# Routing weights kept on chip, gathers paced, row transpositions in the rounded type, and a new order inside the softmax attentions

## The reference

```
x = LN(x + attention(x))          # 16 heads on 4 key heads, softmax            phase "gqa"
x = LN(x + latent_attention(x, ctx)); x = LN(x + ternary_ffn(x))                # "latent", "ternary"
x = LN(x + decayed_linear_attention(x))                                        # phase "decay"
x = LN(x + cross_attention(x, ctx))   # 16 heads, causal softmax                 phase "causal"
x = LN(x + shared_ffn(x) + sum over the 2 best of 8 experts of score[e] * expert_ffn[e](x))   # "shared", "expert"
```

## Time and profile before

| | |
|---|---|
| median of 3 runs | 2088.39 us |
| the profiled execution: its time, its span | 2087.5 us, 2085.7 us |
| mean granted clock of TensorE | 0.967 |
| busy: PE, PEld | 1887.3 us (90%), 1535.6 us (74%) |
| busy: DVE, ACT, POOL | 1041.1 us (50%), 713.2 us (34%), 385.6 us (18%) |
| phases, start of each (us): gqa, latent, causal, shared, expert | 0, 272, about 1298, 1533, 1772 |
| the last TensorE product ends | 2041.0 us |

### The profile page before, as it was taken

The page is one execution under the profiler, slowest core; times in us unless marked ns, Lnnn a source line. Parts: engine busy times, 40 slices in busy tenths (PEclk is TensorE's granted clock), DMA queues, the critical chain, the costliest instruction groups (busy, mean ns, idle before and its releaser), DMA issues. The chain is left out here.

```text
span 2085.7 us, 32789 instructions
## 1 busy us (share of the span) xinstructions
PE 1887.3 (90%) x12124; PEld 1535.6 (74%) x12124; DVE 1041.1 (50%) x1836; ACT 713.2 (34%) x2275; POOL 385.6 (18%) x339
## 2 busy tenths in 40 slices
PE   8899888999999989999899998899879995999991
PEld 6667566788888767777677776677658874899990
DVE  5666753455555446333364547677865332222224
ACT  3555624334444332111231102545632210233332
POOL 1111100000000038000021100001104322745335
PEclk9999999999999999999999999999999998999995
DMA  7110142000000022000093000000015100644257
GB/s 238 42 46 14 43 160 82 1 1 1 1 1 1 1 76 91 1 0 0 24 352 115 1 20 27 26 2 1 2 46 207 46 0 0 243 149 143 82 114 205
DMA packets 73375, 135.89 MB, mean 65 GB/s; under 512 B 13456, under 2 KB 31760, under 8 KB 71184
## 3 DMA queue, kind: packets, MB, share of 16 engines
q1 hardware_dynamic: 47376, 96.28, 13.3%
q0 software_dynamic: 7888, 27.94, 4.5%
q10 hardware_dynamic: 17968, 9.71, 1.8%
HBM read 90.62 MB, written 43.29 MB: 64 GB/s over the span
## 5 line engine op out<-in xcount | busy, mean ns | idle before, releaser
L1473 PE MATMUL banks<-ternary_xth,ternary_wq 128*128 (+1 forms) x352 | 140.6, 399 | 5.0 <-DVE ternary_wq L1404 3.6
L1473 PE MATMUL banks<-ternary_xtl,ternary_wq 128*128 (+1 forms) x352 | 139.4, 396 | 0.0
L97 PE MATMUL banks<-latent_vh,latent_cth 128*128 128x512 f32 x256 | 104.2, 407 | 3.5 <-DVE latent_ctl L1174 3.5
L97 PE MATMUL banks<-weights,expert_xgh 128*128 x312 | 104.7, 336 | 2.4 <-DVE expert_xgl L2086 2.4
L99 PE MATMUL banks<-weights,expert_xgl 128*128 x312 | 101.6, 326 | 0.0
L573 ACT ACTIVATE gqa_pr<-banks,gqa_nb 128x128 f32<-128x128 f32 x256 | 90.4, 390 | 32.6 <-DVE gqa_nb L715 32.6
L98 PE MATMUL banks<-weights,expert_xgh 128*128 x312 | 101.4, 325 | 0.0
L573 ACT ACTIVATE causal_pr<-banks,causal_nb 128x128 f32<-128x128 f32 x256 | 90.4, 395 | 31.1 <-DVE causal_nb L715 31.1
L99 PE MATMUL banks<-latent_vh,latent_ctl 128*128 128x512 f32 x256 | 100.1, 391 | 0.0
L98 PE MATMUL banks<-latent_vl,latent_cth 128*128 128x512 f32 x256 | 100.1, 391 | 0.0
L1433 DVE TENSOR_TENSOR ternary_hf<-ternary_sg,banks 128x512 f32<-128x512 f32 x44 | 30.2, 687 | 135.4 <-issue 79.5
(11 more groups left out here) (462 smaller groups left out, 5412.0 us busy)
## 6 DMA issues: line engine op xcount, KB each, us to landing
x_slots<-decay_zeros SPq DMA_DIRECT2D x39, 256.0 KB, 4.3
y_slots<-decay_zeros SPq DMA_DIRECT2D x39, 256.0 KB, 4.5
y_slots<-expert_ys SPq DMA_DIRECT2D x39, 256.0 KB
expert_xin<-x_slots SPq DMA_DIRECT2D x38, 256.0 KB, 2.9
weights_raw<-in_expert_experts SPq DMA_DIRECT2D x4, 2176.0 KB, 9.2
gqa_tw<-in_ternary_w ACTq DMA_DIRECT2D x4, 2112.0 KB
ternary_raw<-in_ternary_w SPq DMA_DIRECT2D x11, 768.0 KB, 4.1
expert_raw<-in_expert_experts POOLq DMA_DIRECT2D x3, 2176.0 KB, 9.7
```

The costliest lines, as they stand in the source:

```text
L97: pe.matmul(out, wh, xh, start=first, stop=False, **kw)
L1473: a = pe.matmul(dst[:, :], wq[:, j, m, c * P:(c + 1) * P], x[:, c, toks], start=c == 0 and n == 0, stop=c == C - 1 and n == 1)
```

## The change

Scores are no longer scattered: `s_slots`, its zeroing, its 32 scatters in the shared phase and the 39 loads of scores in the expert phase go. ScalarE's `store` copies without a scale, and VectorE multiplies by the score, which is still in SBUF, as it adds a gathered row. For that the lower slots are now gathered into buffers rather than added into `X` by the DMA, with at most two gathers in flight, and VectorE adds them; an upper gather goes into the same buffer and waits until the lower one has been added. The row transpositions of tiles 1 to 38 are done in `F32R`, through an identity that ScalarE rounds at the start of the phase. In the softmax attentions, `rec` and `lo` move ahead of `S`, and `T` (b-1, 1) moves behind `out` (b-2).

```diff
         for b in range(B + 2):
             for h in range(2):
+                if soft and h == 0 and 1 <= b <= B:
+                    plan.append(("rec", b - 1, 0))
+                if soft and h == 0 and b >= 2:
+                    plan.append(("lo", b - 2, 0))
                 if b < B and (h == 0 or not soft):
                     plan.append(("S", b, h))
-                if soft and h == 0 and b >= 2:
-                    plan.append(("lo", b - 2, 0))
...
                 if soft:
-                    if h == 0 and 1 <= b <= B:
-                        plan += [("T", b - 1, 1), ("rec", b - 1, 0)]
                     if h == 0 and b >= 2:
                         plan.append(("out", b - 2, 0))
                     if h == 0 and 1 <= b <= B:
-                        plan.append(("rt", b - 1, 0))
+                        plan += [("T", b - 1, 1), ("rt", b - 1, 0)]
...
-            for n in range(2 * B):
-                at = bass.IndirectOffsetOnAxis(ap=S.pos[:, n:n + 1], axis=0)
-                if n and n % 2 == 0:
-                    pool.wait_ge(scored, 16 * n)
-                pool.indirect_dma_start(S.s_slots, at, S.score[:, n:n + 1], None).then_inc(scored, 16)
-            pool.wait_ge(scored, 16 * 2 * B)
...
             for t in range(B):
-                pool.indirect_dma_start(S.X[:, t, :], None, S.y_slots, slots(t), compute_op=ALU.add).then_inc(low_added[t], 16)
+                if t >= 2:
+                    pool.wait_ge(low_in[t - 2], 16)
+                pool.indirect_dma_start(yg[t], None, S.y_slots, slots(t)).then_inc(low_in[t], 16)
             pool.wait_ge(y_out[(TILES - 1) % 2], 16 * ((TILES - 1) // 2 + 1))
             for t in range(B):
+                pool.wait_ge(low_added, t + 1)
                 pool.indirect_dma_start(yg[t], None, S.y_slots, slots(B + t)).then_inc(yg_in[t], 16)
...
-                act.wait_ge(s_in[i % NX], 16 * (i // NX + 1))
-                act.activation(ys[:, i % 2, :], yb[i % 2], ACT.Copy, scale=sc[:, i % NX:i % NX + 1]).then_inc(y_copied, 1)
+                act.activation(ys[:, i % 2, :], yb[i % 2], ACT.Copy).then_inc(y_copied, 1)
+            act.activation(identr[:, :], S.ident[:, :], ACT.Copy).then_inc(ident_rounded, 1)
...
+            def add_scored(n, k):
+                x = S.X[:, n, :]
+                return dve.scalar_tensor_tensor(out=x, in0=yg[n], scalar=S.score[:, k * B + n:k * B + n + 1], in1=x,
+                                                op0=ALU.mult, op1=ALU.add)
+            for n in range(B):
+                dve.wait_ge(low_in[n], 16)
+                add_scored(n, 0).then_inc(low_added, 1)
...
                     dve.wait_ge(yg_in[n], 16)
-                    dve.tensor_tensor(S.X[:, n, :], S.X[:, n, :], yg[n], ALU.add).then_inc(high_added, 1)
+                    add_scored(n, 1).then_inc(high_added, 1)
...
                 for c in range(C):
-                    m = pe.transpose(tr[:, c * P:(c + 1) * P], x[:, c * P:(c + 1) * P], S.ident[:, :])
+                    cols = slice(c * P, (c + 1) * P)
+                    if i:
+                        m = pe.transpose(tr[:, cols].bitcast(F32R), xin[:, i % NX, cols], identr[:, :])
+                    else:
+                        m = pe.transpose(tr[:, cols], S.first_x[:, cols], S.ident[:, :])
```

More of the change, by code:

```diff
@@ L443, in _ @@
                         sp.dma_start(rows, zeros[:, :]).then_inc(slots_zero, 16)
-                sp.dma_start(S.s_slots.rearrange("(p i) n -> p (i n)", p=P), zeros[:, 0:TILES]).then_inc(slots_zero, 16)
-                sp.wait_ge(slots_zero, 32 * (SLOTS // P) + 16)
+                sp.wait_ge(slots_zero, 32 * (SLOTS // P))
                 sp.dma_start(next_c, S.ctx_dram[:, 0:GT, :]).then_inc(next_c_in, 16)
@@ L1557, in shared_ffn_phase @@
         route_in, given_done, ranked = sem("route_in"), sem("given_done"), sem("ranked")
-        slots_done, rows_done, scattered, scored = sem("slots_done"), sem("rows_done"), sem("scattered"), sem("scored")
+        slots_done, rows_done, scattered = sem("slots_done"), sem("rows_done"), sem("scattered")
         gw_in, gw_zero, first_x_in = sem("gw_in"), sem("gw_zero"), sem("first_x_in")
@@ L1929, in expert_ffn_phase @@
         weh, wel = S.weh, S.wel
-        xin = sb("xin", [P, NX, DM])
+        xin, identr = sb("xin", [P, NX, DM], F32R), sb("identr", [P, P], F32R)
         yg = [raw[t // 8][:, (t % 8) * DM:(t % 8 + 1) * DM] for t in range(B)]
@@ L1935, in expert_ffn_phase @@
         ys = sb("ys", [P, 2, DM])
-        sc = sb("sc", [P, NX])
         six, mv = sb("six", [P, B, 6]), sb("mv", [P, B, 2])
@@ L1945, in expert_ffn_phase @@
         y_out = [sem(f"y_out{b}") for b in range(2)]
-        s_in = [sem(f"s_in{b}") for b in range(NX)]
-        low_added = [sem(f"low_added{b}") for b in range(B)]
+        low_in = [sem(f"low_in{b}") for b in range(B)]
         yg_in = [sem(f"yg_in{b}") for b in range(B)]
-        high_added = sem("high_added")
+        low_added, high_added = sem("low_added"), sem("high_added")
         w_hi, w_ready, tile_done, spare_set = sem("w_hi"), sem("w_ready"), sem("tile_done"), sem("spare_set")
+        ident_rounded = sem("ident_rounded")
         tr_full, tr_hi, tr_lo = sem("tr_full"), sem("tr_hi"), sem("tr_lo")
@@ L1966, in load @@
             def load(i):
-                sp.dma_start(xin[:, i % NX, :], rows(S.x_slots, i)).then_inc(x_in[i % NX], 16)
-            def load_score(i):
-                sp.dma_start(sc[:, i % NX:i % NX + 1], rows(S.s_slots, i)).then_inc(s_in[i % NX], 16)
+                sp.dma_start(f32(xin[:, i % NX, :]), rows(S.x_slots, i)).then_inc(x_in[i % NX], 16)
             for i in range(1, NX):
                 load(i)
-            for i in range(NX):
-                load_score(i)
             for e in (1, 2):
@@ L1983, in _ @@
                 sp.dma_start(rows(S.y_slots, i), ys[:, i % 2, :]).then_inc(y_out[i % 2], 16)
-                if i + NX < TILES:
-                    load_score(i + NX)
             for t in range(B):
@@ L2115, in _ @@
                 if n < B:
-                    dve.wait_ge(low_added[n], 16)
                     dve.wait_ge(yg_in[n], 16)
-                    dve.tensor_tensor(S.X[:, n, :], S.X[:, n, :], yg[n], ALU.add).then_inc(high_added, 1)
+                    add_scored(n, 1).then_inc(high_added, 1)
                 if 1 <= n <= B:
@@ L2141, in transposes @@
                 if i:
+                    pe.wait_ge(ident_rounded, 1)
                     pe.wait_ge(x_in[i % NX], 16 * (i // NX + (i % NX > 0)))
                     pe.wait_ge(tr_lo, i)
-                x = xin[:, i % NX, :] if i else S.first_x
                 for c in range(C):
-                    m = pe.transpose(tr[:, c * P:(c + 1) * P], x[:, c * P:(c + 1) * P], S.ident[:, :])
+                    cols = slice(c * P, (c + 1) * P)
[3 more added lines that the diff above has]
+                        m = pe.transpose(tr[:, cols], S.first_x[:, cols], S.ident[:, :])
                 m.then_inc(tr_full, 1)
@@ L2219, in build @@
         S.landed_at = sb("landed_at", [P, E], U32)
-        S.s_slots = nc.dram_tensor("s_slots", (SLOTS, 1), F32).ap()
         S.ring, S.owner1 = sb("ring", [P, TILES], U32), sb("owner1", [P, TILES], U32)
```

## The result

On one chip the changed kernel took 2092.19 us (median of 13, 2084.73 to 2096.08) and the kernel before 2085.87 (median of 13): ratio **1.0027**, 95% interval 1.0017 to 1.0037. So it is slower by 0.27%, inside the half per cent called "no change" above, but on the other side of zero from the -0.7 us of the sum. The profiled execution of the changed kernel took 2088.54 us with a span of 2086.7 (before: 2087.5 and 2085.7). It lies 3.7 us under its kernel's median and the one of before 1.6 us over its own, so the two traces differ by 1.0 us where the medians differ by 6.3.

What follows compares the result with a forecast made beforehand. TensorE, busy 90% of the span, was taken as the bound; boundary -18.0, its clock -1.0, transpositions -3.8, order +16.1 and its clock +6.0 gave -0.7 on 2087.5: 2086.8 us, forecast as 2087, range 2060 to 2102.

Steps and rivals of the forecast that it cites:

- the sum: All priced terms added, against the profiled 2087.5 us: -18.0 - 1.0 - 3.8 + 16.1 + 6.0 = -0.7 us.
- The boundary: Between shared and expert phase: without POOL's score scatters, TensorE's 20.9 us stall falls to about 3 us, -18.0 us.
- the transpositions: Expert phase: four row transpositions in the rounded type take 0.34 us for 0.44, over 38 tiles -3.8 us.
- what hides: Score loads, zeroing of `s_slots`, ScalarE's copy without a scale and its identity rounding: hidden beside other work, 0.
- the clock behind the boundary: Start of the expert phase: less half clock after the shorter stall, -1.0 us (between 0 and -2.7).
- the rule for weight loads: Expert transpositions: loading 128 columns takes 107 ns, so no saving and 3.8 us longer; as a rival 0.14, 2090.6 us.
- The mechanism of the order: Softmax phases: 22.5 us of waits for the spread go; TensorE waits for `rts` and the probabilities' copy instead.
- the first path: Softmax steps: late `T` delays the second-half exponentials that overwrite what it reads, and `rts` with them, by 1.8 us.
- the size of the order in the attentions: Both softmax phases: +16.1 us of waits (ends -22.5 and +24) and +6.0 us of clock (0 to +12).
- the seven that the sum had priced: Softmax k and v steps and gqa's 11: new stalls of about 3 us, priced within the +6.0 us of clock.
- 10.6: Steps 12 to 15 of both softmax phases, without projections to cover the copy: 10.6 us for 10.0, +4.8 us.
- POOL's new waits are met early: At the end, POOL's waits before the upper gathers are met 1 to 6 us early, costing 0.

Runs made afterwards that it cites:

- e8: The changed kernel with the expert phase's row transpositions back in plain float32: 2093.55 us, ratio 1.0055 to the kernel before.
- e1: The changed kernel with the old order of the softmax phases, all else as changed: 2064.41 us, ratio 0.9881 to the kernel before.
- e5: The changed kernel with a third buffer in the causal phase, so second-half exponentials don't wait for `T`: 2075.81 us, ratio 0.9953 to the kernel before.
- e3: The changed kernel with `T` (b-1, 1) back ahead of `out`, `rec` and `lo` still ahead of `S`: 2048.19 us, ratio 0.9791 to the kernel before.
- e14: The changed kernel with `T` (b-1, 1) behind `out` only from step 12 on: 2070.55 us, ratio 0.9945 to the kernel before.
- e13: The changed kernel with `T` (b-1, 1) behind `out` only in steps 1 to 11: 2074.79 us, ratio 0.9964 to the kernel before.
- e15: The changed kernel itself, run again beside e13 and e14: 2088.31 us, ratio 1.0026 to the kernel before.
- e2: The kernel before with the new order of the softmax phases and nothing else: 2122.14 us, ratio 1.0153 to the kernel before.
- e9: The changed kernel with seven of VectorE's 16 lower sums put between the last three expert tiles: 2086.54 us, ratio 1.0024 to the kernel before.
- e11: The changed kernel with the edits of e3 and e9 together: 2047.68 us, ratio 0.9833 to the kernel before.

## Why the prediction was wrong, and where it was right

**The boundary, the transpositions and what hides: right.** -18.8 us for -18.0; the stretch of the experts -4.0 for -4.8, of which e8 puts 3.2 on the type, for 3.8, and 0.8 is left for the clock behind the boundary, for 1.0. Together that is -22.8 for -22.8. One transposition now takes 0.29 / 4 = 0.073 us in the chain, and the first product behind pays 0.07, so 0.34 for four was right as a net (0.36) and not as a duration. The trace speaks against the rule for weight loads of the Trainium skill, "TensorE: Matmul & The Clock Gate", section "LDWEIGHTS (loading the stationary operand)", that the prediction weighed (0.107 us each). The zeroing, the loads and the copy without a scale cost nothing that can be seen. All but the order is e1: -25 us for -22.8, and in its trace 1.9 of them are a short end.

**The mechanism of the order: right.** The waits for the spread went; `T` behind `out` came to the steps as foretold: causal k steps 6 and 10 take 16.9 us (16.8), v step 7 15.9 (15.8), gqa steps 3 and 7 19.6 and 19.2 (19.7); causal steps 2 and 3, at 18.2 and 16.9, are longer. e5 shows the first path by taking it away, e3 shows that the two halves of the edit are worth opposite signs.

**The step that failed: the size of the order in the attentions**, +16.1 of waits and +6.0 of clock in the sum. In the pair of traces it is 25.7: 21.3 of idle for 16.1, and 4.5 of clock for 6.0. Only the first is sure, since the other five executions with this order have 20.1 to 21.3 of idle too, and clock from 0.5 to 14.9. So the waits were priced 4 to 5 us too low, and with them the forecast stood just below zero instead of above it. By kind of step, changed minus before (us):

| | in the sum | length | idle | busy |
|---|---|---|---|---|
| gqa 1 to 11 | +1.8 | +0.3 | +2.5 | -2.2 |
| gqa 12 to 14 | +3.0 | +6.3 | +2.7 | +3.6 |
| gqa 15 and end | +3.0 | +4.0 | +2.4 | +1.6 |
| causal 1 to 11 | +3.5 | +7.1 | +8.6 | -1.5 |
| causal 12 to 14 | +1.8 | +3.4 | +2.2 | +1.2 |
| causal 15 and end | +3.0 | +4.4 | +3.3 | +1.2 |

(What stands ahead of step 1 makes up the rest, 0.3.) Behind step 11 the waits are as priced, 10.5 us for 10.8. They were priced too low in the steps with projections, where the idle time grew by 11.1 and the sum had 5.3, in causal above all; the busy time fell by 3.7 us there. And the clock was lost elsewhere than priced: behind step 11 the products take 7.5 us longer. In gqa that is partly what follows the stall of step 11, one of the seven that the sum had priced (0.50 from 211 to 216 us), and partly what follows the waits for the copy, for which it had no clock (0.63 from 225 to 229).

Steps 12 to 14 of gqa as windows, before and changed:

```profile
213.99:244.06 30.07, 26.23 (x232) 18.40 (x228) 24.33 (x42) 22.09 (x104) 3.97 (x6) 1.00 0.27 68
213.28:249.62 36.34, 29.84 (x233) 20.60 (x229) 25.56 (x42) 23.26 (x106) 3.48 (x6) 0.88 0.20 48
```

The steps 12 to 14 take 13.5, 11.1 and 11.8 us in gqa and 10.7, 11.5 and 11.3 in causal, where 10.6 was foretold; the terms given for the 10.6 add up to 10.45. The timeline of gqa step 14 has it, for the earlier trace rows:

```profile
240.82 0.47 PE L97 MATMUL banks<-gqa_woh,gqa_oth 128*128 128x512 f32 x1 [0.66 <-DVE gqa_otl L738]
243.66 1.03 PE L875 MATMUL banks<-ident,gqa_pr 128*128 128x128 f32 x8
...
245.71 1.22 DVE L726 COPY gqa_pt<-banks 128x1024 f32<-128x1024 f32 x1
...
247.07 1.06 PE L875 MATMUL banks<-ident,gqa_pr 128*128 128x128 f32 x8 [1.95 <-DVE gqa_pt L726]
...
248.07 1.62 PE L891 MATMUL banks<-gqa_pt,gqa_v 128*32 128x512 f32 x8
```

The copy stands behind the statistics and `T` (b, 0) waits 1.95 us for it, as said; `pv` behind that wait takes 1.62 us for 1.07 in step 13; and the wait for `lo`, put at 0.15 us, is 0.66 in this step (there is none in step 13), since everything that `lo` needs (`rts`, the normalised output, its copy) has moved back with the late `T`. 21.9 us of the late `T` lie in the steps with projections and 18.1 behind them (e14 and e13 against e15).

**What was not in the sum at all** is the end. Without the blocked issue it is about 2 us shorter than before (42.8 and 43.1 for 45.1), and with it 2.4 longer. In both short ones the first upper gather could start 3.6 and 3.7 us after TensorE's last product, for 5.6 before; that the paced gathers let the last y tile land sooner is the likely reason, but no run tests it. "POOL's new waits are met early" was true; that VectorE's burst would hold POOL's issue itself was not thought of.

The sum said -0.7 and the two traces differ by +1.0: the order +3.6, the end +2.4, the untouched phases -4.2. The medians differ by +6.3, and the 5.3 us between are what the two profiled executions lie off their medians, which no term explains.

**What stays open.** The order costs 30 to 32 us in the runs. The traces find 25 to 27 of them in the softmax phases (25.5 in e2; 26.8 and 25.4 in the changed kernel and e15, against e1) and the rest outside: 7.0 in e2's shared phase, 4.4 in the end, which was blocked in the changed kernel's profiled execution and not in e1's. How often the end is blocked in the runs without a profile is not known, nor what sets the clock's part. And why the same burst blocked the gather in 11 executions and not in two is open, at the same distance of 5.79 us from the burst's start in the changed kernel and in e15.

## What to carry to other kernels

An edit that moves one operation for the sake of another is two edits: here half of it (the reciprocal ahead of the scores) gained 14 us, and the other half (the transposition behind the output product) lost about 40. Before moving a reader of a buffer later, follow who overwrites the buffer and whose bank that writer's engine frees next. And look first at the steps in which no other work covers the chain: a quarter of the steps held nearly half of the loss. When one trace is held against another, take TensorE's idle and busy time apart: here the idle time of a stretch came back within 1.2 us from execution to execution, and the busy time within 14 us.

## What the runs showed of the hardware

VectorE's unbroken burst of sums with two SBUF operands held the issue of one indirect gather on POOL for 4.2 to 5.8 us in 11 of 13 executions, and in all 11 until 0.82 us after the burst. The two or three lower gathers issued during the same burst took 0.94 to 1.53 us; why they were let through is not shown. With the burst over before the gather, it took 0.95 us (e9, e11). The Trainium skill, "SBUF — State Buffer", section "SBUF: two separate sides", says of the port pair that VectorE and GpSimd share that it is an exclusive lock held for one instruction, that a VectorE operation with two SBUF inputs takes it against a GpSimd one that reads SBUF, and that the loser waits. The trace agrees that VectorE's sums can hold POOL back. It does not agree that the wait lasts one instruction: in the changed kernel it spanned seven of 0.67 us. The two executions without it are explained by neither.

A float32 transposition of 128 columns took 0.11 us and one in the rounded type 0.073, with 0.07 us more for the first product behind the four.

The same stretch of the same code differs from execution to execution by its busy time, with the granted clock. In six executions with the new order TensorE's idle time in the softmax phases was 86.1 to 87.3 us, its busy time 443.8 to 458.1 (e8 and e9).
